# Both waits of a head pair ahead of its first matmul, in the causal attention of a post-layernorm transformer layer

## The reference, cut to what matters

```
# x: [16, 2048, 1024] float32; 16 heads of 64; feed-forward width 4096
Q, K, V = split_heads(x @ Wq.T), split_heads(x @ Wk.T), split_heads(x @ Wv.T)
Q, K = rope(Q), rope(K)
logits = einsum('bhnd,bhmd->bhnm', Q, K) / sqrt(64)
probs = softmax(where(causal, logits, -inf))
attn = einsum('bhnm,bhmd->bhnd', probs, V)
x = layernorm(x + merge_heads(attn) @ Wo.T)
h = gelu(x @ binarize(w1).T + b1)        # binarize: row mean of |w| times sign(w)
x = layernorm(x + h @ binarize(w2).T + b2)
```

## Time and profile before

| what | value |
|---|---|
| time, median of 3 runs | 3604.47 us (3602.34 to 3748.36) |
| the profiled execution's own time | 3603.93 us |
| its span, slowest core (core 5) | 3602.2 us |
| spans of the 8 cores | 3587.9 to 3602.2 us |
| PE busy | 2525.6 us (70%) |
| ACT busy | 1506.6 us (42%) |
| DVE busy | 1007.7 us (28%) |
| attention of the two sequences | about 308 to 1096 us and 1324 to 2134 us |

### The profile page before, as it was taken

How to read it: one execution, slowest core, us unless ns; L and a number is a source line. 1 busy time by engine, 2 the same in 40 slices (tenths; PEclk the granted TensorE clock), 3 DMA queues, 4 the chain that set the end, 5 groups by cost and what they waited for, 6 DMA issues and landing times.

```text
span 3602.2 us, 33813 instructions; the slowest of 8 cores (3587.9 to 3602.2 us)
## 1 busy us (share of the span) xinstructions
PE 2525.6 (70%) x11026; PEld 1019.0 (28%) x11026; DVE 1007.7 (28%) x1392; ACT 1506.6 (42%) x2402; POOL 233.0 (6%) x375
## 2 busy tenths in 40 slices
PE   2996676877866977576768843119697797887976
PEld 0442121222223432122212212114343343333432
DVE  0664333222124653322221145110201202112022
ACT  0555363755843545364738825232213123122130
POOL 0000000000000000000000001111120110201101
PEclk9996667777778985667777765559898898998988
DMA  7100101000001110101010035342332422324213
GB/s 132 39 27 4 44 10 43 9 21 31 3 31 65 42 41 12 43 11 43 3 49 4 3 117 158 117 137 92 116 94 80 134 90 95 100 97 132 89 52 94
DMA packets 68826, 225.36 MB, mean 63 GB/s; under 512 B 12210, under 2 KB 16306, under 8 KB 67634
## 3 DMA queue, kind: packets, MB, share of 16 engines
q0 software_dynamic: 32960, 117.46, 11.7%
q1 hardware_dynamic: 35698, 105.74, 8.7%
HBM read 185.42 MB, written 41.94 MB: 63 GB/s over the span
## 4 chain that ended last, share of the span: by engine, by line
PE 57%; DVE 13%; ACT 12%; issue 9%; DMA 7%; another core or an unknown queue 1%; SPq 1%; DVEq 0%; POOL 0%; ACTq 0%; POOLq 0%
PE psA L603 7%; PE psB L907 6%; PE psA L939 6%; PE psE L907 6%; PE psA L270 5%; PE psB L573 5%; PE psE L573 5%; DMA RS<-xs 4%; PE psA L492 4%; PE psE L939 3%; PE psB L939 3%; ACT RB L626 3%; ACT RS L646 2%; DMA RW<-w 2%; PE psA L614 2%
## 5 line engine op out<-in xcount | busy, mean ns | idle before, releaser
L626 ACT ACTIVATE RB<-psA,kn 128x512 bf16<-128x512 f32 (+3 forms) x1280 | 711.1, 626 | 296.8 <-PE psA L603 176.5
L603 PE MATMUL psA<-RQ 64*128 64x512 bf16 (+3 forms) x1280 | 375.2, 440 | 221.6 <-ACT RB L626 212.2
L907 PE MATMUL psB<-RW,RQ 128*128 128x512 bf16 x1024 | 265.9, 407 | 121.6 <-ACT RW L914 110.6
L492 PE MATMUL psA<-RW,RB 128*128 128x512 bf16 x512 | 180.3, 515 | 173.9 <-DVE RS L504 142.9
L958 DVE TENSOR_TENSOR RS<-psA,b2s 128x1024 f32<-128x1024 f32 x16 | 18.9, 1220 | 921.6 <-PE psE L939 921.6
L939 PE MATMUL psA<-RW 128*128 128x512 bf16 x1024 | 262.8, 379 | 7.4 <-ACT RW L914 7.4
L573 PE MATMUL psE<-RB,RQ 128*65 128x512 bf16 (+3 forms) x640 | 244.0, 462 | 24.7 <-ACT RB L626 23.0
L270 PE MATMUL psA<-RW,RB 128*128 128x512 bf16 x1024 | 229.2, 382 | 41.9 <-DMA RW<-woT 28.6
L603 PEld LDWEIGHTS psA<-RQ 64*128 64x128 bf16 x1280 | 89.2, 97 | 573.7 <-issue 562.9
L907 PE MATMUL psE<-RW,RQ 128*128 128x512 bf16 x1024 | 249.9, 388 | 0.0
L573 PE MATMUL psB<-RB,RQ 128*65 128x512 bf16 (+3 forms) x640 | 237.3, 449 | 9.9 <-ACT RB L626 8.3
(11 more groups left out here) (144 smaller groups left out, 2884.2 us busy)
## 6 DMA issues: line engine op xcount, KB each, us to landing
RW<-bw2s POOLq DMA_DIRECT2D x256, 256.0 KB, 2.9
RS<-xs SPq DMA_DIRECT2D x64, 512.0 KB, 4.0
x2s<-RS SPq DMA_DIRECT2D x32, 512.0 KB, 2.9
RW<-w POOLq DMA_DIRECT2D x32, 512.0 KB, 5.6
RW<-w POOLq DMA_DIRECT2D x8, 2048.0 KB, 9.6
RS<-x2s SPq DMA_DIRECT2D x16, 512.0 KB, 6.2
bw2s<-RB POOLq DMA_DIRECT2D x32, 256.0 KB, 3.5
RW<-x2s SPq DMA_DIRECT2D x16, 512.0 KB, 7.8
```

The lines of the kernel that those rows point to most:

```text
L492: bank=bank: e.matmul(bank, attn_sup[:, hp * 512 + j * 128: hp * 512 + (j + 1) * 128], wo_b[:, hp * 1024 + piece * 512: hp * 1024 + (piece ...
L603: coff=coff, qw=qw: e.matmul(psA[:, sl * 512 + coff:sl * 512 + qw], k_fm[e64:e64 + 64, hp * S + k * 128:hp * S + (k + 1) * 128], q_fm[e64: ...
L626: k=k, hh=hh, qw=qw: e.activation(pt_sb2[k % 2][:, eh * 512 + coff: eh * 512 + qw], psA[:, sl * 512 + coff:sl * 512 + qw], AF.Exp, bias=mb ...
L907: e.matmul(ps[:, q0:q1], bw1T[:, dc * FF + fc * 128: dc * FF + (fc + 1) * 128], x2_fm[:, dc * SUP + q0:dc * SUP + q1], start=(dc == 0), st ...
```

## The change

The waits of the two score matmuls are all put ahead of the first one (`ww0`), and the second one has none of its own. In the same way the product with V of head 0 waits for the exponentials of both heads, and that of head 1 for nothing. The number of instructions, their shapes and their order on each engine stay as they are.

```
-                            ww = [psA_user.get(sl)]
-                            if Ts == 0 and hp == 0 and k == 0 and eh == 0:
-                                ww += p1_end + [m13]
+                        ww0 = [psA_user.get(sa), psA_user.get(sb)]
+                        if Ts == 0 and hp == 0 and k == 0:
+                            ww0 += p1_end + [m13]
...
+                            ww = ww0 if eh == 0 else ()
                             stmm[eh] = kb.op(
...
                         if k > 0:
-                            emit_pv(0, k - 1, prev_ex[0])
-                            emit_pv(1, k - 1, prev_ex[1])
+                            emit_pv(0, k - 1, [prev_ex[0], prev_ex[1]])
+                            emit_pv(1, k - 1, None)
...
-                    pvm0 = emit_pv(0, nk - 1, prev_ex[0])
-                    pvm1 = emit_pv(1, nk - 1, prev_ex[1])
+                    pvm0 = emit_pv(0, nk - 1, [prev_ex[0], prev_ex[1]])
+                    pvm1 = emit_pv(1, nk - 1, None)
```

## The result

The changed kernel takes 3639.4 us (median of 9 runs), the kernel before 3605.1 us (median of 10). The ratio is 1.0095, with a 95% interval of 1.0084 to 1.0106: 34 us more. The forecast was 3645.4 us, 41 us more than the kernel before.

What follows compares the result with a forecast made beforehand. ACT was taken to set the pace of wide steps at clock 1.00, PE at 0.50. The sum was 3603.9 + 18.2 + 17.9 + 3.4 + 2 = 3645.4 us, with a forecast range of 3627 to 3668.

Steps and rivals of the forecast that it cites:

- Part 1: Wide steps at clock 1.00: a closed score-exponential loop takes 1.32 us against 1.16; 114 steps x 0.16 = +18.2 us.
- Part 2: Last products with V of a block: head 0's starts 0.28 us later, hidden by nothing; 64 blocks, +17.9 us.
- Part 3: Second step of a block: the product with V waits for both exponentials, +0.07 us in each of 48 blocks, +3.4 us.
- plus 0.14: Second step of a block: exponentials end at 717.33, plus 0.14 us gives the product's start, 717.47 against 717.41.
- Part 4: All else: +2 us (0 to 6) for wide steps at clock 0.50; band and its products with V 0.
- The 2 us for wide steps at clock 0.50: Wide steps at clock 0.50: new loop of 1.53 us just equals PE's pace; 0.02 us added for some 100 steps.
- The band, put at 0: Band steps: the pair starts where head 1 starts today, and waiting products lie under the next exponential wait: 0.
- A: Wide steps at clock 1.00: freed PE time reaches the end, 31 us less, 3573 us; chance 0.06.
- B: Attention: PE no longer keeps clock 1.00 inside a block, slower by over 2%, 3701 us, +2.7%; chance 0.11.
- C: Nothing changes: moved waits are mostly met when PE comes to them and hand-overs overlap, 3604 us; chance 0.07.
- rule on matmuls of different row groups: Score pairs: matmuls on different row groups run at once, so pairing gives PE time back in each wide step.
- rule on repeating gaps: Wide steps: too few PSUM buffers, three slots for two per step, so ACT should pause in each step; size 0.16 us.

Runs made afterwards that it cites:

- e1_scores: Against the kernel before, only the score matmuls have both waits ahead; the products with V wait as before: 1.0038, +14 us.
- e2_end: Against the kernel before, only the last product with V of head 0 in each block waits for both exponentials: 1.0045, +16 us.
- e5_pv_second: Against the kernel before, only the products with V of a block's first step, run in its second, have both waits ahead: 1.0023, +8 us.
- e3_pvloop: Against the kernel before, only the products with V inside the loop have both waits ahead: 1.0042, +15 us.
- e4_scores_nowide: Against the kernel before, score matmuls have both waits ahead except in wide steps from a block's third on; products with V as before: 1.0015, +5 us.
- f1_four_pair: Against the kernel before, scores get a fourth slot where no output projection is pending, with score waits grouped, products with V as before: 0.9863, -50 us.
- f3_four_before: The kernel before with a fourth score slot where no output projection is pending, each matmul keeping its own wait: 0.9861, -50 us.

## Why the prediction was right, point by point

Time and sign came out: +34 us against +41, inside the forecast's own range. The attention took 1436.1 us before and 1471.2 after (both sequences, mean of the eight cores), and the count splits these 35.0 us so: wide steps from the fifth of a block on +14.3, the change of block (48 of them) +12.6, second and third steps +7.1, fourth steps -5.3, the band from the fifth step on +2.2, the first block group +0.9, and the blocks that hold an output projection +3.1. The last figure holds their share of each part. By the steps of the prediction:

**Part 1, the loop in wide steps at clock 1.00: right.** Forecast 1.32 us a round, found 1.30. The loop's three links in the trace of the changed kernel, as medians over all such steps: 0.144 us from the exponential's end to the score matmul, 0.470 from there to the next exponential (I had 0.39 + 0.10 = 0.49), 0.687 for that exponential. The wide steps took 14.3 us more in the count; scaled from 0.16 to the measured 0.146 a step, 114 steps are 16.6 us, against 18.2 in the forecast. e1_scores shows the same loop without the rest of the change.

**Part 2, the last product of a block: right.** 0.26 us a block instead of 0.28, 16.6 us instead of 17.9; e2_end has it alone.

**Part 3, the second step: the mechanism was right, the size was not.** The third step's score pair starts 0.14 us later (2.48 us after the block's first exponential instead of 2.34, medians), double my 0.07. The step that was off is "plus 0.14": I had let the product start 0.14 us after the exponential's end, and it starts 0.25 us after it (medians of all such blocks). This product has a second wait, for DVE to have read the tile two blocks earlier (`aev_prev`). DVE has long done so, but the wait stands behind the one for the exponential in PE's own order and takes its turn only then (the last section shows the rows). By e5_pv_second this is 8 us alone, against 3.4 in the forecast.

**Part 4, all else: one term that did not come, two missing, and one of the other sign.** The 2 us for wide steps at clock 0.50 did not come: their median is 1.533 us before and 1.534 after. The band, put at 0, costs 0.02 us a step (1.464 to 1.483 us for its first step at 1.00, median), at most 5 us in all. The waits of the products in wide steps do cost something, as e3_pvloop shows, but not on top of part 1: the loop through the products needs 1.22 us a step on average, that through the slots 1.30, and only the slower one is paid. In the count the wide steps have +6.9 us in e3_pvloop, +14.2 in e1_scores and +14.3 in the whole change. The three parts of the change alone add up to 14 + 16 + 15 = 45 us, and together they take 34; these 6.9 us are the larger part of the difference, and the rest is within the intervals of the three runs. On the other side, in 5 of 42 blocks the fourth step already ran at 1.00 (before, none was as short), and these steps took 5.3 us less in all; the same is seen in e1_scores (-5.5) and e4_scores_nowide (-2.8) and not in e2_end or e3_pvloop. With the grouped score waits PE has both score matmuls of the second step behind its pause between blocks, and not one of them ahead of it. f1_four_pair bears this out in part: its score waits are grouped too, but with four slots both matmuls are done ahead of the pause, and none of its fourth steps is as short as those five (2.3 to 2.4 us instead of 3.4). That this is what brings the clock back earlier is still argued, since no run moves this one matmul alone. That part 3 was forecast 3.7 us too small and the fourth steps took 5.3 us off is luck: two misses that offset each other in part.

**The rivals.** A (the freed PE time reaches the end) is refuted: the pairing did free PE time, 82 us of PE's busy time by the page, and with four slots grouped and single waits have medians 0.5 us apart. B (the clock) is refuted too: the granted clock over the span is 0.783 before and after in the mean of the eight cores, and steps at either level are as long as their loops say. C (nothing) is outside the interval of the ratio. The Trainium skill's rule on matmuls of different row groups ("TensorE: Matmul & The Clock Gate", Part 3) holds in the trace, 0.39 us for two, and is worth nothing here, since another engine sets the pace. The Trainium skill's rule on repeating gaps ("Perfetto Trace Analysis", Identifying Performance Opportunities), that they can mean too few PSUM buffers, was the better guide, and the trace agrees: giving the scores a fourth slot was worth 50 us. The kernel before had shown the sign of it, the pauses of 0.20 to 0.25 us in its band, and I had read them as a cost already paid.

## What to carry to other kernels

Before waits are grouped, ask for each of them what the early half of the work did with its head start: here the head start of one score matmul was what kept the exponentials without a pause. Write the round trip down as a loop, link by link, and compare it with the pace of the engine that sets the time; of several such loops only the slowest is paid, so parts that each cost something alone need not add up. And where a loop of this sort already binds in one part of the kernel, as in the band here, try a further buffer slot before another order of waits: f1_four_pair and f3_four_before, at 0.986 of the time before, beat both kernels.

## What the runs showed that I had not expected

A wait that has long been met still costs PE time when it stands behind one that has not. The product with V of a block's first step waits for ACT and for DVE. In the changed kernel (DVE's last reading of the tile `psB`, and the products that write to it next):

```profile
711.16 0.67 DVE L706 SCALAR_TENSOR_TENSOR RB<-psB,RS 64x512 bf16<-64x512 f32 x1
...
726.11 1.03 PE L573 MATMUL psB<-RB,RQ 128*65 128x512 bf16 x2
```

DVE ended at 711.83, 14 us earlier. Yet the product starts 0.25 us after the exponentials' end (724.60 + 1.26 = 725.86). The count has 1.516 against 1.266 us after the block's first exponential, as medians. In one of ten such blocks (`hp` 1 in the last two groups) the program leaves the DVE wait out, since an earlier one covers it, and there the product starts 0.144 us after the exponentials' end, in the changed kernel as in e5_pv_second. So the met wait costs 0.1 us.

And a delay of 0.1 us in PE's order can come back as an alternating pace, 1.16 and 1.26 us, so a mean over steps shows neither of the two.
